# Queries kept in SBUF and their rests made by GpSimd; the two heads' scores staggered by one matmul, with an exponential for each head

## The reference

```
h = ln(x, g1, be1);  x = attn(h, h, Wq1, Wk1, Wv1, Wo1, bo1) + x      # self-attention, 16 heads of 64
h = ln(x, g2, be2);  x = attn(h, context, Wq2, Wk2, Wv2, Wo2, bo2) + x # cross-attention, 64 keys
h = ln(x, g3, be3);  y = h @ Wp + bp;  a, gate = y[:, :1024], y[:, 1024:]
x = a * gelu(gate) @ W2 + b2 + x
attn: q, k, v = h Wq, c Wk, c Wv by head;  softmax(q k^T / 8) v, heads side by side, @ Wo + bo
```

## Time and profile before

| What | Value |
|---|---|
| median of 3 runs | 1985.43 us (1984.62 to 1986.59) |
| the profiled execution's own time | 1986.85 us |
| its span | 1985.1 us |
| TensorE's granted clock | 1.00 of full speed |
| chunk loop of the first attention | about 61 to 1463 us of the span |

### The profile page before, as it was taken

How to read it: one execution, slowest core, us unless ns; L and a number is a source line. 1 busy time by engine, 2 the same in 40 slices (tenths; PEclk the granted TensorE clock), 3 DMA queues, 4 the chain that set the end, 5 groups by cost and what they waited for, 6 DMA issues and landing times.

```text
span 1985.1 us, 32079 instructions
## 1 busy us (share of the span) xinstructions
PE 1971.6 (99%) x12056; PEld 1345.1 (68%) x12056; DVE 1393.6 (70%) x2382; ACT 1150.6 (58%) x2042; POOL 1444.1 (73%) x752
## 2 busy tenths in 40 slices
PE   9999999999999999999999999999999999999999
PEld 7555655667565556755655666565569999888888
DVE  6688687666768786587687666767867888744443
ACT  6665576565556665465666555656756766533332
POOL 3699899978979997899799798979896665200000
PEclk9999999999999999999999999999999999999999
DMA  7301000011000000020000001010030420000100
GB/s 256 138 38 64 17 22 22 12 33 54 22 12 12 33 12 33 1 75 11 11 12 22 33 12 54 22 33 1 22 106 22 150 65 1 1 22 33 33 11 32
DMA packets 40506, 77.63 MB, mean 39 GB/s; under 512 B 5920, under 2 KB 29600, under 8 KB 38304
## 3 DMA queue, kind: packets, MB, share of 16 engines
q1 hardware_dynamic: 40352, 75.59, 11.5%
HBM read 51.46 MB, written 24.12 MB: 38 GB/s over the span
## 4 chain that ended last, share of the span: by engine, by line
PE 92%; DVE 3%; POOL 3%; issue 1%; ACT 1%; POOLq 0%; DVEq 0%
PE score L577 21%; PE score L556 18%; PE score L703 9%; PE attn_project L512 8%; PE attn_project L688 5%; PE attn_project L717 5%; PE score L524 5%; PE score L658 4%; PE score L626 3%; PE attn_project L538 3%; PE first_score L538 3%; PE score L562 3%; POOL acc L1528 2%; PE first_score L672 1%; PE first_score L588 1%
## 5 line engine op out<-in xcount | busy, mean ns | idle before, releaser
L1528 POOL TENSOR_TENSOR acc<-acc,pT 128x1024 f32<-128x1024 f32 x384 | 916.7, 2387 | 54.4 <-POOL acc L1528 0.9
L1271 ACT ACTIVATE pT<-score 128x1024 f32<-128x1024 f32 x512 | 515.7, 1026 | 89.1 <-PE score L562 53.5
L556 PE MATMUL score<-qk 64*128 64x512 f32 x3072 | 467.5, 405 | 2.5 <-DVE hT L852 1.9
L577 PE MATMUL score<-pT,vT 128*64 128x512 f32 x1952 | 432.3, 595 | 0.0
L556 PEld LDWEIGHTS score<-qk 64*128 64x128 f32 x3072 | 267.2, 184 | 97.0 <-ACT pT L1271 20.9
L907 DVE TENSOR_REDUCE nmax<-first_score 128x2 f32<-128x1024 f32 x256 | 311.0, 1215 | 2.4 <-PE first_score L538 2.4
L907 DVE TENSOR_REDUCE nmax<-attn_project 128x2 f32<-128x1024 f32 x256 | 311.0, 1215 | 1.0 <-PE attn_project L538 0.9
L577 PEld LDWEIGHTS score<-pT,vT 128*64 128x64 f32 x1952 | 134.7, 137 | 259.5 <-issue 252.6
L1525 POOL TENSOR_TENSOR acc<-pT 128x1024 f32<-128x1024 f32 x64 | 153.4, 2396 | 68.6 <-ACT pT L1271 68.6
L512 PE MATMUL attn_project<-hT,wqk 128*128 128x512 f32 x738 | 186.3, 401 | 0.0
L703 PE MATMUL score<-hT,wp 128*128 128x512 f32 x768 | 183.7, 395 | 0.0
(11 more groups left out here) (201 smaller groups left out, 3007.2 us busy)
## 6 DMA issues: line engine op xcount, KB each, us to landing
wqk<-wqk_parts SPq DMA_DIRECT2D x24, 512.0 KB, 3.3
xres<-x_middle SPq DMA_DIRECT2D x10, 512.0 KB, 3.7
raw_v<-in_L_xattn_Wv SPq DMA_DIRECT2D x8, 512.0 KB, 4.9
keys_all<-keys SPq DMA_DIRECT2D x1, 4096.0 KB, 13.1
values_all<-values SPq DMA_DIRECT2D x1, 4096.0 KB, 13.2
wqk_parts<-wqk SPq DMA_DIRECT2D x8, 512.0 KB, 3.3
out_x<-xres SPq DMA_DIRECT2D x7, 512.0 KB, 3.0
xres<-in_x SPq DMA_DIRECT2D x3, 1024.0 KB, 5.7
```

The lines of the kernel that those rows point to most:

```text
L556: last = e.matmul(bank, key_part(P, h, r, jt), queries1[P % 2][r, w, c * BANK:(c + 1) * BANK], start=(fresh and part == 0), stop=(not fres ...
L577: last = e.matmul(banks[bank][head * DH:(head + 1) * DH, :], vT[:, v_slot(D, jt), c0:c0 + DH], pT[:, jt, head, :], start=(jt == 0), stop=( ...
L1271: e.activation(pT[:, jt].rearrange("p h n -> p (h n)"), SC[R % 2][:, :], ACT.Exp).then_inc(s.exponential, 1)
L1528: e.tensor_tensor(total, total, pT[:, jt], ALU.add).then_inc(s.probs_added, 1)
```

## The change

Queries: except for the first three units, ScalarE now copies the scaled queries from the PSUM bank in fp32 into the place of their rest (`queries_kept`, which alone frees the bank); one chunk later it rounds them from SBUF (`round_queries`), and GpSimd subtracts in place (`split_queries`), at the end of its part of the chunk. Scores: head 1 is issued one matmul behind head 0, also across the tiles; each head's exponential is an instruction of its own over 128 x 512 and frees its own half of the score banks.

```diff
+        queries_whole = [tile[:, N:2 * N] for tile in (qk0_whole, qk1_whole)]      # fp32 over the rests
+        FIRST_QUERIES = [(0, 2), (0, 3), (1, 2)]
+        def queries_unit(C):
+            P, c = divmod(C, CHUNKS)
+            return [(P + 1 + c, 3 - c)] if C >= 0 and P + 1 + c < B * PAIRS else []
...
     # TensorE
-                free[bank] = ((s.split_lo, qk_of[P, u]),)
+                free[bank] = ((s.split_lo, keys_of[P, u]) if u < 2 else queries_rest((P, u)) if (P, u) in FIRST_QUERIES
+                              else (s.queries_kept, queries_of[P, u] - len(FIRST_QUERIES)),)
...
-                    free[f"S{R % 2}" + "ab"[head]] = ((s.exponential, R + 1),)
+                    free[f"S{R % 2}" + "ab"[head]] = ((s.exponential, 2 * R + head + 1),)
...
-                    for part in range(len(TERMS) + (jt % TPC < 2)):
-                        for head in range(2):
-                            score(TILES * C + jt, part, head)
+                    parts = len(TERMS) + (jt % TPC < 2)
+                    for part in range(parts):
+                        score(TILES * C + jt, part, 0)
+                        if part:
+                            score(TILES * C + jt, part - 1, 1)
+                        elif jt and C + 1 < NC:
+                            first_score(*next_part(C + 1, jt - 1), 1)
                     if C + 1 < NC:
-                        for head in range(2):
-                            first_score(*next_part(C + 1, jt), head)
+                        first_score(*next_part(C + 1, jt), 0)
+                    score(TILES * C + jt, parts - 1, 1)
+                if C + 1 < NC:
+                    first_score(*next_part(C + 1, TILES - 1), 1)
...
     # VectorE, whole_array
-                    if job[0] == "qk":
-                        split_qk(*job[1:])
+                    if job[0] == "qk" and job[2] < 2:
+                        change_keys(*job[1:])
...
     # ScalarE
+                        e.activation(queries_whole[P % 2][:, span], banks[bank], ACT.Copy, scale=SCALE
+                                     ).then_inc(s.queries_kept, 1)
+            def round_queries(P, u):
+                span = slice((u - 2) * BANK, (u - 1) * BANK)
+                need.wait_ge(s.queries_kept, queries_of[P, u] - len(FIRST_QUERIES))
+                e.copy(queries1[P % 2][:, 0, span], queries_whole[P % 2][:, span]).then_inc(s.queries_hi, 1)
...
-                e.activation(pT[:, jt].rearrange("p h n -> p (h n)"), SC[R % 2][:, :], ACT.Exp
-                             ).then_inc(s.exponential, 1)
+                e.activation(pT[:, jt, head, :], banks[f"S{R % 2}" + "ab"[head]], ACT.Exp).then_inc(s.exponential, 1)
...
                 if C + 1 < NC:
                     make_shift(C + 1)
+                for unit in queries_unit(C - 1):
+                    round_queries(*unit)
                 write_oT(C)
...
     # GpSimd
+            def split_queries(P, u):
+                span = slice((u - 2) * BANK, (u - 1) * BANK)
+                need.wait_ge(s.queries_hi, queries_of[P, u])
+                e.tensor_tensor(queries1[P % 2][:, 1, span], queries_whole[P % 2][:, span],
+                                queries1[P % 2][:, 0, span].bitcast(F32), ALU.subtract).then_inc(s.queries_lo, 1)
...
                     if C == NC - 1 and jt in (2, 4):
                         scale_oT(C - 3 + jt // 2)
+                for unit in queries_unit(C - 1):
+                    split_queries(*unit)
```

More of the change, by code:

```diff
@@ L140, in block_kernel @@
             ("wo1", [PAIRS, DIM], F32R))
+        _, qk1_whole, _, qk0_whole = overlay(
+            ("before_qk", [PRING * N + 3 * TILES * BANK + (2 * ARING + 1) * BANK], F32), ("qk1_whole", [4 * N + BANK], F32),
+            ("sums_between", [2 * BANK], F32), ("qk0_whole", [4 * N + BANK], F32))
         PAIR = BANK // 2
+        queries_whole = [tile[:, N:2 * N] for tile in (qk0_whole, qk1_whole)]
         queries1 = [tile[:, 0:2 * N].rearrange("p (w n) -> p w n", w=2) for tile in (qk0, qk1)]
@@ L287, in block_kernel, with queries_rest @@
         keys_of = numbered((P, u) for P in range(B * PAIRS) for u in range(CHUNKS))
+        queries_of = numbered((P, u) for P in range(B * PAIRS) for u in range(2, 2 + CHUNKS))
+        FIRST_QUERIES = [(0, 2), (0, 3), (1, 2)]
+        def queries_rest(unit):
+            if unit in FIRST_QUERIES:
+                return s.first_queries_lo, queries_of[unit]
+            return s.queries_lo, queries_of[unit] - len(FIRST_QUERIES)
         def rows_there(key):
@@ L549, in score @@
                 if part < len(TERMS):
-                    for u in (2 + c, jt // TPC):
-                        need.wait_ge(s.split_hi, qk_of[P, u])
-                        need.wait_ge(s.split_lo, qk_of[P, u])
+                    need.wait_ge(s.queries_hi, queries_of[P, 2 + c])
+                    need.wait_ge(*queries_rest((P, 2 + c)))
+                    need.wait_ge(s.split_hi, keys_of[P, jt // TPC])
+                    need.wait_ge(s.split_lo, keys_of[P, jt // TPC])
                     if part == 0:
@@ L570, in attend @@
                 need.wait_ge(s.v_copied, TILES * D + jt + 1)
-                need.wait_ge(s.exponential, R + 1)
+                need.wait_ge(s.exponential, 2 * R + 2)
                 bank = products_bank(C)
@@ L1245, in split_qk @@
                 if u >= 2:
-                    e.activation(queries1[P % 2][:, 0, (u - 2) * BANK:(u - 1) * BANK], banks[bank], ACT.Copy, scale=SCALE
-                                 ).then_inc(s.split_hi, 1)
+                    span = slice((u - 2) * BANK, (u - 1) * BANK)
+                    if (P, u) in FIRST_QUERIES:
+                        e.activation(queries1[P % 2][:, 0, span], banks[bank], ACT.Copy, scale=SCALE
+                                     ).then_inc(s.queries_hi, 1)
+                    else:
+                        e.activation(queries_whole[P % 2][:, span], banks[bank], ACT.Copy, scale=SCALE
+                                     ).then_inc(s.queries_kept, 1)
                     return
@@ L1262, in copy_v, with exponential @@
                 e.copy(vT[:, v_slot(D, jt), :], banks[bank]).then_inc(s.v_copied, 1)
-            def exponential(R):
+            def exponential(R, head):
                 jt = R % TILES
-                need.wait_ge(s.scored, 2 * R + 2)
+                need.wait_ge(s.scored, 2 * R + head + 1)
                 need.wait_ge(s.keys2_stored, 16)
@@ L1419, in _ @@
                 for jt in range(TILES):
-                    exponential(TILES * C + jt)
+                    for head in range(2):
+                        exponential(TILES * C + jt, head)
                 if n == BC - 7 and b + 1 < B:
```

17 lines of the change are left out of this document (8 added, 9 removed).

## The result

The changed kernel takes 2000.56 us (median of 4 runs, 2000.35 to 2001.78) against 1986.01 us for the kernel before (4 runs, 1984.62 to 1988.19): a ratio of 1.0074, interval 1.0056 to 1.0091. That is slower by 0.7%, 14.6 us, where +7.2 was forecast. The profiled execution took 2000.35 us, span 1998.6 us, 13.5 more than before in both.

The account below looks back on a forecast made before the run. TensorE was taken as the bound, with VectorE pacing the score stage and GpSimd the second bound. 4.7 (chunk forms) + 0.5 (lag stall) + 2.0 (loop's end) = +7.2 on 1985.43, so 1992.6 us, range 1989.5 to 1997.

Parts of the forecast that it names:

- rival B: GpSimd's lag stalls already at 11: 4 us in the first chunks, 2 per three batch rows; 2002 us, chance 0.13.
- 4.7 + 0.5 + 2.0: The forecast's sum in us: chunk forms up to chunk 56, one GpSimd lag stall, and the loop's end; +7.2.
- the forms: Kinds of chunk by how the score stage starts, each with its own shift; together +4.7 us up to chunk 56.
- Together +0.13 a chunk: Normal chunk's score stage: first reduction 0.11 earlier, a matmul slot at the end costing 0.24; net +0.13 us.
- The chunks with an idle VectorE at the start: Seven chunks (18, 19, 34, 35, 50, 51, 62): the reduction comes 0.23 later, the attends +0.31 us.
- the like of chunk 61: Seven chunks (13, 14, 29, 30, 45, 46, 61) where head 1's bank comes late: forecast -0.34 us each.
- Rival A: Score matmuls of the two heads run free of each other, so no slot is lost: 1978 us, faster, chance 0.2.
- +2.0 on the chain that ends the loop: GpSimd's adds from chunk 56 on: +0.95, less 0.2 for earlier exponential halves, +1.25 for one more subtraction.
- what was costed at nothing: Two exponentials for one (taken as 1.0 us, under VectorE's 1.13 pace) and ScalarE's extra rounding copy: no cost.
- Exponential 5 ... binds: GpSimd's subtraction delays adds and so the next chunk's exponentials; free below lag 14.4, one 0.5 us stall after chunk 6.
- It comes round in each of three batch rows: GpSimd's lag from chunk 19: 11.2, plus 0.4 in each of 20 to 23, to 12.8; no stall, recurring each row.

Follow-up runs that it names:

- stagger_only: Against the kernel before: head 1 one matmul behind and an exponential per head, all queries split by VectorE from the bank as before; 2001.48 us, ratio 1.0077.
- fold_first: The whole change, with VectorE in chunk 63 folding chunk 62's sums before splitting the cross-attention keys; 1999.61 us, ratio 1.0063 to the kernel before.
- exps_only: The kernel before with only an exponential for each head, scores in pairs and queries as before; 1984.99 us, ratio 0.9997.
- queries_only: Against the kernel before: only the queries' part (kept in SBUF, rounded later, rests by GpSimd), scores in pairs, one exponential for both heads; 1995.92 us, ratio 1.0048.
- vector_late_exps: Against the kernel before: queries kept in SBUF, rests by VectorE behind its fold, scores in pairs, an exponential per head; 1972.33 us, ratio 0.9928.

## Why the prediction was right in direction and half the size

The direction was right. The size was not: 14.6 us measured for 7.2, outside the 1989.5 to 1997 given to the forecast and in the band of rival B. In the trace, against 4.7 + 0.5 + 2.0, stand 4.2 for the forms, 6.3 for the stalls, 2.1 for GpSimd's end, 1.5 behind it that the sum did not have, and -0.7 ahead of the loop.

**Right: the forms of the chunk.** "Together +0.13 a chunk" was measured as 19.63 - 19.49 = 0.14, first reduction 1.78 (forecast 1.80), attends 9.40 (9.4). The chunks with an idle VectorE at the start came out +0.31 (chunk 18: 9.08 to 9.39), the like of chunk 61 -0.31 to -0.35. Up to chunk 56 the forms gave 4.2 where 4.7 was summed; chunks 1 to 3 gained 0.3 each in length, not 0.11, and chunk 4 lost 0.13. (The same terms without rounding on the way make 4.6.) The two experiments that take one half of the sum each bear it out: 0.24 for the slot at the end (stagger_only), 0.11 back from the start.

The part rested on matmuls of the two heads keeping the order of issue, read from chunk 61; after the change the same shows at 917.81 and 918.15, and stagger_only has no gain at all. Rival A, at 0.2, is out. By the Trainium skill, "TensorE: Matmul & The Clock Gate", section "Part 3: Packing small matmuls — row/col tiling", matmuls of different tiles start and end in program order and only weight loads are pulled ahead; the traces agree with that, and the rule about independent tiles that the prediction weighed as rival A does not reach past a matmul that waits.

**Right: the end.** "+2.0 on the chain that ends the loop": GpSimd's last add came 2.1 behind chunk 56's shift, its chunk took 100.04 / 5 = 20.0. Another 1.5 us behind it was not in the sum. It came from a wait that the prediction did not look at: in chunk 63 TensorE stands 3.18 us for the fold behind VectorE's key splits, and is then late where GpSimd alone should have set the end. fold_first brings these 1.5 us back.

**Right: what was costed at nothing.** Two exponentials of a tile take 1.08 to 1.09, within the 1.0 to 1.2 given and below VectorE's pace of 1.13; exps_only shows no loss. ScalarE's wait ahead of `write_oT` is still there (109.3 us in all, 126.1 before).

**The step that failed: GpSimd's subtraction.** "Exponential 5 ... binds ... a lag under 14.4 ... a stall of 0.5 once". It measured 6.3 us, in chunks 5, 6, 7, 13, 14 and 15. Three things in it were wrong. (19.6 + 7.4 - 12.5 is 14.5, not 14.4; nothing hangs on it.)

First, who waits. I had the attends wait for the exponentials of their own tiles, and took tile 7's as harmless since its attend comes last. But the first attend needs its output bank, and that is half of tile 6's score bank, so it waits for tile 6's exponential, which waits for add 6 of the chunk before. Add 6 ends at lag + 15.1, the attends follow 0.65 later, so they start at lag + 15.75 less the chunk before's length, if that is later than 9.40. With 19.63 this gives 13.3 as the largest free lag. It holds in numbers: chunk 7 by chunk 6's row 15.89 + 15.75 - 20.00 = 11.64, measured 11.69; chunk 15 by chunk 14's 15.90 + 15.75 - 20.45 = 11.20, measured 11.27. (For chunk 5 it gives 10.09 and 10.60 was measured: the adds of chunk 4 took 0.5 longer than the 17.5 in it.) In the later batch rows the lag reached 13.01, 13.26 and 12.99 (chunks 23, 39, 55) and cost nothing. The formula holds for the attends; in chunk 14 it gives no wait (14.42 + 15.75 - 21.29 = 8.88), and there the lag shows in the scores before them: the first reduction comes at 2.57, and at 2.31 in chunk 30. Which wait carries it there was not followed up. The run with the products in tile 7's bank confirms the cause for the attends.

Second, how fast the lag grows. I started from chunk 6's 9.41 and added 5 x 1.12 to get 15.0; it reached 15.89 although 1.23 of it had already been paid in chunk 5, so 2.1 were missing. 1.2 of them are TensorE's: chunks 1 to 3 are 0.3 shorter each and not 0.13 longer, which a GpSimd that is behind has to make up too. The other 0.9 are GpSimd's: its first add of chunk 0 stands 7.90 behind TensorE's start and not 7.43, and the seven adds of chunks 1 and 4 took 18.4 and 18.0 us, 18.1 and 17.8 before.

Third, where. "It comes round in each of three batch rows" counted from chunk 18 on; chunks 8 to 15 carry weight splits on GpSimd as well, and the lag went from 4.83 to 15.90 there. The trace of before had it in plain sight: 9.53 in chunk 12.

Rival B named the right mechanism (the lag, which stalls by late exponentials) at the wrong threshold, 11, and gave 2002; it had 0.13. The measured 2000.56 is 1.4 from B and 8.0 from the forecast, but B's nearness is partly luck: it put 4 us of stalls in the first chunks and 2 in each of three later batch rows, and they came as 6.3 in the first row and none later, where the forecast's "no stall" was right.

**The rivals' side.** No gain was to be had in the way the change was built: queries_only shows that without the stagger GpSimd paces the loop at 20.0 us, and stagger_only that with it the loop is longer whatever GpSimd does.

## What to carry to other kernels

Before work is moved to an engine, compare its work per stage with the length of the stage after the change: 0.73 us of slack does not hold 1.25, and the debt grows until it meets a buffer. To find where it meets it, follow not only who reads the late buffer but whose output bank is freed by its reader. Staggering two interleaved streams costs one slot at the end of each stage that another engine paces; freeing banks by halves and starting the pacing engine earlier paid, in pairs and with the moved work in a stretch where its own engine waits.

## What the runs showed of the hardware that was not expected

**A VectorE instruction with two SBUF inputs beside GpSimd's adds.** The three splits of chunk 63 (a fourth follows the fold) took 0.72, 1.78 and 2.87 us in the kernel before (sorted by length), and 1.75, 2.69 and 2.88 in the changed one: one operation of 128x512, with a factor of four between its ends. The late subtractions, of the same size, took 1.59 (chunk 38) and 2.69 (chunk 26), and 0.65 to 2.78 over all 61. GpSimd suffers as well, in the same stretch:

```profile
1462.82 1.71 POOL L1577 TENSOR_TENSOR oT<-oT,sums 128x512 f32<-128x512 f32 x1
1464.49 2.79 POOL L1568 TENSOR_TENSOR acc<-pT 128x1024 f32<-128x1024 f32 x1
```

against 1.29 and 2.39 undisturbed. The Trainium skill, "GPSIMD Engine Reference", section "1. Specifications", has the two engines share their SBUF interfaces, with contention for VectorE instructions with two SBUF inputs; the traces agree and give the size. The split whose other input is in PSUM took 0.68 to 0.69 in all 62 cases of the kernel before, GpSimd busy beside 49 of them.

The slow instruction behaves like one that waits. In vector_late_exps 58 of the 61 subtractions start while a GpSimd instruction runs, and each of these takes what is left of that instruction and 0.54 to 0.58 more. For chunk 38's, which starts at 905.44, this was running:

```profile
904.11 2.37 POOL L1568 TENSOR_TENSOR acc<-acc,pT 128x1024 f32<-128x1024 f32 x1
```

1.04 us of it are left, and 1.04 + 0.55 = 1.59. The three that start just after a GpSimd instruction has ended take 0.65. The add behind such a subtraction takes 2.62 to 2.81 in place of 2.37. The splits of chunk 63 follow the same count: the 1.75 starts when 1.20 of a GpSimd instruction are left. So the cost depends on where in GpSimd's instruction VectorE's starts.

**TensorE's clock at the end.** Windows of the changed kernel around the idle stretch of chunk 63 (length, busy times as above, then the granted clock):

```profile
1463.10:1466.30 3.20, 0.02 (x2) 0.02 (x1) 3.20 (x4) 0.71 (x2) 3.20 (x2) 0.84 0.00 0
1466.30:1470.00 3.70, 3.70 (x16) 2.61 (x18) 2.75 (x4) 1.27 (x3) 3.56 (x2) 0.50 0.02 4
```

In and behind 3.2 us with hardly a matmul TensorE's granted clock fell to 0.50, the 1.2 GHz level, and it was 0.50 over the whole second window. With the fold first (no idle) the clock is 1.00 there. That execution got 0.50 elsewhere: for 3.41 us in chunk 7, behind 0.83 us of waiting in front of the attends, which then took 1.5 us longer, and for 3.41 us from 1450.46 on, in chunk 62, which took 20.06 us in place of 18.36. The trace of the whole change waits the same 0.83 in chunk 7 and keeps 1.00, so two executions of the same instructions differ there by 1.5 us.
